# The ones and shift rows of two graph attentions on TensorE: 128 partitions in place of three

## The reference, cut to what matters

```
e = leaky_relu(as_n[src] + ad_n[dst], 0.2)
m = segment_max(e, dst)
p = exp(e - m[dst])
s = segment_sum(p, dst)
alpha = p / (s[dst] + 1e-16)
out = segment_sum(alpha[:, :, None] * h[src], dst)
```

## Time and profile before

| | |
|---|---|
| median of three runs | 4101.87 us (4100.34 to 4104.19) |
| profiled execution, its own time | 4104.02 us |
| its span | 4102.4 us |
| PE busy | 3794.5 us (92%) |
| DVE, ACT, POOL busy | 1965.1, 1702.3, 1577.8 us |
| mean granted TensorE clock | 0.968 of 2.4 GHz |
| wide stage, first add to last | from 622.6 us to about 1208 us |
| narrow stage, first add to last sum | from 1764.8 us to about 2211 us |

### The profile page before, as it was taken

How to read it: one execution, slowest core, us unless ns; L and a number is a source line. 1 busy time by engine, 2 the same in 40 slices (tenths; PEclk the granted TensorE clock), 3 DMA queues, 4 the chain that set the end, 5 groups by cost and what they waited for, 6 DMA issues and landing times.

```text
span 4102.4 us, 58268 instructions
## 1 busy us (share of the span) xinstructions
PE 3794.5 (92%) x18463; PEld 2939.7 (72%) x18473; DVE 1965.1 (48%) x2784; ACT 1702.3 (41%) x2902; POOL 1577.8 (38%) x1201
## 2 busy tenths in 40 slices
PE   8998769999988989679998999999999999989998
PEld 4554436777768889512223799999999999965588
DVE  7245787666633444699984333323223222013334
ACT  1114776666652321278995233333333333300021
POOL 3887885444420000001111244444444444357600
PEclk9999989999999999889999999999999999999999
DMA  4333112222223321221112355555555554369801
GB/s 142 101 105 74 37 22 63 65 71 74 59 79 106 100 69 55 100 81 58 51 45 94 105 183 181 180 184 184 184 182 182 180 184 138 111 229 303 266 17 63
DMA packets 204684, 483.10 MB, mean 118 GB/s; under 512 B 71582, under 2 KB 87989, under 8 KB 204566
## 3 DMA queue, kind: packets, MB, share of 16 engines
q1 hardware_dynamic: 115638, 201.96, 15.2%
q0 software_dynamic: 54368, 185.24, 14.6%
q10 hardware_dynamic: 34560, 94.45, 6.6%
HBM read 357.64 MB, written 123.55 MB: 117 GB/s over the span
## 4 chain that ended last, share of the span: by engine, by line
PE 43%; POOL 5%; DVE 5%; issue 3%; ACT 1%; DMA 0%; SPq 0%; DVEq 0%; ACTq 0%; POOLq 0%
PE ps L1913 29%; POOL work L1995 5%; PE ps L1245 3%; PE ps L1901 3%; PE ps L1587 3%; DVE work L1125 2%; PE ps L306 2%; PE ps L298 1%; DVE work L1153 1%; PE ps L1218 1%; ACT work L1308 1%; PE ps L324 0%; DMA work<-msg_d,work 0%; ACT ps L1299 0%; DVE mask L1762 0%
## 5 line engine op out<-in xcount | busy, mean ns | idle before, releaser
L1913 PE MATMUL ps<-wsplit,xsplit 128*128 x6840 | 1235.6, 337 | 1.3 <-POOL xsplit L1880 1.3
L1913 PEld LDWEIGHTS ps<-wsplit,xsplit 128*128 128x128 f32 x6840 | 1180.2, 188 | 1.5 <-issue 1.5
L1308 ACT ACTIVATE work<-ps,work 128x418 f32<-128x418 f32 x720 | 435.9, 607 | 239.7 <-PE ps L1218 238.8
L1255 PE MATMUL ps<-hbuf,work 128*128 128x193 f32 x2400 | 494.5, 345 | 13.2 <-DVE work L1170 13.1
L1880 POOL TENSOR_TENSOR xsplit<-ct,xsplit 128x768 fp32r<-128x768 f32 x190 | 368.8, 1941 | 298.5 <-ACTq L1945 298.4
L1153 DVE SCALAR_TENSOR_TENSOR work<-work,cnt 128x1250 f32<-128x1250 f32 x240 | 370.6, 1544 | 228.7 <-ACT work L1308 224.8
L1850 DVE CAST wsplit<-wplain 128x768 fp32r<-128x768 f32 x204 | 115.2, 565 | 760.3 <-PE ps L1913 742.3
L1950 ACT ACTIVATE ct<-ps,invs 128x768 f32<-128x768 f32 x190 | 171.5, 903 | 710.1 <-PE ps L1913 710.1
L1255 PEld LDWEIGHTS ps<-hbuf,work 128*128 128x128 f32 x2400 | 385.3, 191 | 83.4 <-issue 83.4
L1299 ACT ACTIVATE ps<-work,lr 128x418 f32<-128x418 f32 x720 | 418.5, 607 | 6.1 <-DMA work<-lrow_d 6.1
L1875 POOL DMA_INDIRECT ct<-x_d,relrec x190 | 198.5, 1045 | 516.9 <-PE ps L1901 497.0
(11 more groups left out here) (219 smaller groups left out, 4351.7 us busy)
## 6 DMA issues: line engine op xcount, KB each, us to landing
wplain<-in_L_gnn_W_rel SPq DMA_DIRECT2D x34, 2304.0 KB, 9.6
msg_d<-ct ACTq DMA_DIRECT2D x190, 384.0 KB, 2.6
work<-lrow_d SPq DMA_DIRECT2D x47, 625.0 KB, 3.8
feat_d<-work ACTq DMA_DIRECT2D x30, 386.0 KB, 3.4
hbuf<-feat_d SPq DMA_DIRECT2D x60, 193.0 KB, 2.5
gat_d<-work POOLq DMA_DIRECT2D x12, 960.0 KB, 5.2
xplain<-gat_d SPq DMA_DIRECT2D x30, 384.0 KB, 3.3
work<-xa_d SPq DMA_DIRECT2D x27, 384.0 KB, 3.2
```

What stands on the lines that cost most here:

```text
L1255: last = pe.matmul(ps[:, self.b0 + b, t * (C + 1):(t + 1) * (C + 1)], p[:, dt * P:(dt + 1) * P], self.feat(h, s), start=(s == 0 and t == 0 ...
L1308: act.activation(self.p[q % 3][:, c0:c1], ps[:, b, 0:c1 - c0], ACT.Exp, bias=self.l2[:, col:col + 1], scale=1.0 - SLOPE)\
L1913: last = pe.matmul(ps[:, 4 + 2 * (u % 2) + h, 0:HALF], x[:, u, c * P:(c + 1) * P], w[:, bass.ds(base + (c * D + h * HALF), HALF)], start=( ...
```

## The change

The stationary operand becomes 128 x 128 of ones, and `crow` gets 128 partitions, of which the DMA still fills the first three. The others are zero: DVE sets both `crow` buffers to zero once, at the beginning of each attention stage. The product is the same.

```diff
-                self.ones3 = cv(P, BF16, 3)
+                self.ones128 = cv(P, BF16)
                 self.parts = cv(32, BF16)
                 self.turned = [cv(32, BF16) for _ in range(2)]
-                self.crow = [cv(NP, BF16, 3) for _ in range(2)]
+                self.crow = [cv(NP, BF16) for _ in range(2)]
@@ def shift(h), on SP
-                    sp.dma_start(self.crow[h % 2], shift_d[h]).then_inc(self.s_c_in[h % 2], 16)
+                    sp.dma_start(self.crow[h % 2][0:3, :], shift_d[h]).then_inc(self.s_c_in[h % 2], 16)
@@ def dve, ahead of the stage's first maximum
                 step.count(v.memset(self.parts, 0.0))
-                step(v.tensor_copy(self.ones3, ones[0:3, :]))
+                for row in self.crow:
+                    step.count(v.memset(row, 0.0))
+                step(v.tensor_copy(self.ones128, ones[:, :]))
@@ def add(q), on PE
-                        pe.matmul(ps[:, b, 0:c1 - c0], self.ones3, self.crow[h % 2][:, c0:c1], start=False, stop=True,
+                        pe.matmul(ps[:, b, 0:c1 - c0], self.ones128, self.crow[h % 2][:, c0:c1], start=False, stop=True,
                                   skip_group_check=True).then_inc(self.s_add, 1)
```

## The result

The changed kernel takes 3983.9 us (median of four runs, 3980.95 to 3988.18) against 4102.1 before: a ratio of 0.9713, interval [0.9701, 0.9725]. The forecast was 3982 us. The profiled execution has a span of 3981.7 us, 120.7 less than before.

What follows compares the result with a forecast made beforehand. PE was taken to bound the wide stage, with PE, DVE and ACT close in the narrow one. From the profiled execution, 4104.0 - 110 + 3 + 1.2 - 14 = 3984.2 us; forecast median 3982 us, range 3966 to 4030.

Steps and rivals of the forecast that it cites:

- Whose pause it is: PE around each add: some 0.31 us of pauses come from three-row contraction height beside 128, not from bf16 beside fp32.
- The price of an add: PE, wide stage: an add falls from 0.49 to 0.18 us, a unit to 3.77 us, 110 us over 118 units.
- the start's loss: First six wide units: DVE's two maxima and one product take some 4.5 us per unit, giving 3 us back.
- The other engines in the wide stage: Wide stage: ACT 86% and DVE 84% busy after the change, leaving PE the bound.
- The narrow stage: Narrow stage: 14 us gained, 8 in the middle and 6 at the end, with bounds of 0 and 25.
- The memsets: DVE zeroing both `crow` buffers: 0.6 us each, 1.2 us on the wide stage's path, 0 in the narrow stage.
- The cast: DVE's cast behind the wide stage's memsets: same 128 columns per partition, so the same cost as before.
- Only in part: Rival, 11%: each add's 0.099 us weight load stays exposed, an add costs 0.28 us, the whole 4022 us.
- Nothing goes: Rival, 6%: pauses belong to accumulating into a bank ACT wrote, or to the add's semaphore; 4103 us.
- dearer: Rival, 4%: pauses stay and the 128-row load's 0.099 us is exposed after each; wide unit 5.0 us, whole 4143 us.

Runs made afterwards that it cites:

- runs at 64 and 65 rows: Changed kernel with the add's operands on 64 or 65 partitions instead of 128: ratios to the kernel before 1.0003 and 0.9723.
- the adds in a row: Kernel before, three rows kept, with the wide stage's three adds per unit one behind the other after the 5th matmul: 4072.2 us, ratio 0.9869.
- the fp32 bias: Changed kernel, with the first product's one-row fp32 bias (L357) also given 128 rows: 3976.4 us, ratio to the kernel before 0.9697.
- run with short maxima: Changed kernel with DVE's narrow-stage maxima over 625 of 1250 columns, half the targets left out: 3945.7 us, ratio to the kernel before 0.9626.
- 32 rows: Changed kernel with the add's operands on 32 partitions instead of 128: ratio to the kernel before 0.9995.
- the narrow stage alone: Changed kernel with 128 rows in the narrow stage only, three in the wide one: 4086.1 us, ratio to the kernel before 0.9963.
- all together: Changed kernel with 128-row bias, finished heads' columns on DVE, and starting maxima two and one per unit in turn: 3977.4 us, ratio to the kernel before 0.9702.
- the columns on DVE: Changed kernel with the narrow stage's work on finished heads' columns moved from POOL to DVE, fused into two instructions: 3982.2 us, ratio to the kernel before 0.9715.

## Why the prediction was right

- **Whose pause it is.** The step that carried all was to read the 0.31 us as the price of a change of height, from two places in the trace with the type held and the height held. The runs at 64 and 65 rows, the adds in a row and the fp32 bias each bear it out.
- **The price of an add** was put at 0.18 us and measures 0.18. The wide unit was forecast at 3.77 us and takes 3.80: eight fp32 instructions take 1.31 us, not 1.29. With the start's loss the stage was to give 107 us; it gave 105.7. That is so close by luck: at 0.895 us per unit in place of 0.93 the steady part gave 4 us less than forecast, and the late rise of the clock in the execution before gave up to 2.7 back.
- **The other engines in the wide stage.** ACT and DVE were to be 86 and 84% busy, and are 84 and 81.
- **The start** was rightly put down to DVE's two maxima per unit, at 4.5 us of DVE for each. In the changed kernel's profiled execution PE waits for DVE there once, 2.0 us, and the granted clock falls to half behind that wait. Where the clock rose later, PE has four short waits in place of it, one each 4.41 us, and no fall (PE in the run with short maxima, whose wide stage is that of the changed kernel):

```profile
642.51 0.92 PE L1259 MATMUL ps<-hbuf,work 128*128 128x193 f32 x4 [0.83 <-DVE work L1154]
...
646.92 0.92 PE L1259 MATMUL ps<-hbuf,work 128*128 128x193 f32 x4 [0.34 <-DVE work L1154]
```

  Either way the first head takes 49.0 us: DVE sets it, whenever the clock rises. With 32 rows it takes 55.36, with the clock rising at 10.2 us as against 9.1 in the run with short maxima: 6.4 us between them, close to the 9.3 less 3 that were forecast.
- **The narrow stage** was to give 14 us out of 0 to 25, by DVE's idle time in the middle and ACT's at the end. It gave 16.5, some 11 in the ten heads with maxima (8 was forecast) and 5.4 in the last two (6). DVE rose to 96% (97 was forecast) and PE fell to 83 (80). What I didn't see is that PE's waits there would cost clock.
- **The memsets** were priced at 0.6 us each and take 0.64 (1.27 for the two, 1.15 more on the way to the first add); in the narrow stage they are hidden, as said. The cast did not cost the same, as I had taken it: its record fell from 0.62 to 0.16 us, for a reason that no run shows. The Trainium skill's one cycle per element (VectorE: DVE Perf Modes, Zero memsets can be issued as uint32) gave 1.3 for both and agrees.
- **The rivals.** *Only in part*: an exposed weight load would have left 0.28 us per add; there are 0.18, and the add's load starts while the matmul ahead of it streams (PE and its loads, after, the matmuls of L1258 and the load under them):

```profile
850.64 0.65 PE L1258 MATMUL ps<-hbuf,work 128*128 128x193 f32 x3
...
850.97 0.10 PEld L1221 LDWEIGHTS ps<-work 128*128 128x128 bf16 x1
...
851.13 0.34 PE L1221 MATMUL ps<-work 128*128 128x416 bf16 x1
```

  By these rows the other rule of the Trainium skill that I weighed (TensorE: Matmul & The Clock Gate, The mechanism: a load overlaps a matmul in flight only if their row groups differ) doesn't hold for neighbours of the same height; another sentence of that section, which lets a load into the background weight buffer go ahead, fits them. *Nothing goes* and *dearer* are excluded by the same rows.

The 3982 us against 3983.9 is closer than the terms deserve: their errors, 4 us too much in the steady part of the wide stage, up to 2.7 too little at its start, 2.5 too little in the narrow stage, and 2.5 of scatter ahead of them, partly cancel.

## What to carry to other kernels

A matmul whose contraction is low costs nothing less for being low, and in a stream of full-height matmuls it costs about 0.3 us more at full clock (0.2 ahead, 0.1 behind; 0.2 and 0.2 in fp32). Look for it from start to start, since the records' ends hide it; then raise the operand above 64 partitions with zeros, or pick the row with a column of the identity, or at least put the low matmuls side by side so that they share one pause. Where PE bounds the stretch the gain is the whole pause; where it doesn't, read the next engine's idle time and expect no more than that.

## What the runs showed of the hardware that was not expected

**Short waits of PE cost clock in the narrow stage.** Before the change the granted clock there was full from 1780 us on. After it, it falls now and then to 1.2 GHz for some 3 us. One such place, in the changed kernel (PE's timeline, then the windows with PE first and the granted clock third from the end):

```profile
1752.08 0.34 PE L1221 MATMUL ps<-work 128*128 128x416 bf16 x1
1754.77 1.07 PE L1248 MATMUL ps<-work,hbuf 128*65 128x512 f32 x2 [2.36 <-DVE work L1153]
...
1755.98 1.91 PE L1248 MATMUL ps<-work,hbuf 128*65 128x512 f32 x2
```

```profile
1754.00:1756.00 2.00, 1.23 (x4) 0.49 (x5) 2.00 (x2) 1.01 (x2) 2.00 (x1) 0.93 0.00 0
1756.00:1758.00 2.00, 2.00 (x4) 0.59 (x3) 2.00 (x3) 0.61 (x1) 1.70 (x2) 0.50 0.00 0
```

The two instructions of one matmul of 512 columns, which take 1.02 us elsewhere, take 1.91. Counted in stretches of 10 us, leaving out the stage's start and end, the changed kernel has three with a clock below 0.985. The more of them an execution has, the longer its narrow stage: with three it took 424.1 us (and 424.2 with the 128-row bias), with six 425.9 (the narrow stage alone), with seven 426.7 (all together), with eight 427.9 (the columns on DVE), with ten 432.6 (65 rows, on another chip). The one with short maxima has none. A wait of PE isn't enough to bring it about, as the 2.72 us at 1787.02 were followed by full clock. What decides it is left open.

**An instruction of POOL with two operands held DVE's product up for nearly its own length.** Beside POOL's 1.32 us at 1752.08, DVE's product took 2.63 us in place of 1.46, and so, within 0.01 us, at six more of the stage's heads. A maximum that began beside POOL's one-operand instruction took 1.97 us in place of 1.46; yet a product that began beside such an instruction at 2040.29 took its 1.46 us. So the kind of instruction on both sides counts, and these rows don't show the rule:

```profile
1752.08 1.32 POOL L1093 TENSOR_TENSOR work<-work,mask 128x640 f32<-128x640 f32 x1 [27.60 <-DVEq L1173]
1752.09 2.63 DVE L1153 SCALAR_TENSOR_TENSOR work<-work,cnt 128x1250 f32<-128x1250 f32 x1
1753.49 2.89 POOL L1094 TENSOR_SCALAR work<-work 128x640 f32<-128x640 f32 x1
1754.64 1.97 DVE L1125 CUSTOM_DVE_ANT_0 work<-ct,work 128x1250 f32<-128x1250 bf16 x1
```
